# A conditioned attention and expert layer on one core: expert products spread one per step behind the scores, and one mask product per head

## The reference

```
x = x + attention(layernorm(x), ...)        # 16 heads of 64, one shared key and value head
x = x + experts(x, ...)                     # 8 experts of 128, the best 2 per token, and a shared one of 256

attention:  q = l2norm(xn @ Wq) * q_scale;  k = l2norm([null_k, xn @ Wk]) * k_scale
            sim = 8 * q @ k.T + relative position bias
            sim = -max where key > query, and where mask is false
            out = layernorm(softmax(sim) @ [null_v, v] @ Wout)

experts:    y = sum over the 2 chosen experts of weight * (leaky(x @ Wgate) * (x @ Wup)) @ Wdown
            y = y + the same without a weight for the shared expert (two blocks of 128)
```

## Time and profile before

| | |
|---|---|
| three runs | 1165.67, 1167.64, 1169.62 us |
| the profiled execution | 1168.08 us, span 1166.3 us |
| PE busy | 1052.0 us, 90% of the span |
| DVE busy | 776.0 us, 67% |
| ACT busy | 526.6 us, 45% |
| POOL busy | 443.6 us, 38% |
| mean granted PE clock | 0.972 |

### The profile page before, as it was taken

One profiled execution on the slowest core, in us unless ns is written; L12 is line 12 of the kernel. 1 busy time (PEld: TensorE's weight loads), 2 busy tenths in 40 slices (PEclk: granted clock), 3 DMA queues, 4 the chain that ended last, 5 costly groups with the idle time before them and its releaser, 6 DMA issues.

```text
span 1166.3 us, 23102 instructions
## 1 busy us (share of the span) xinstructions
PE 1052.0 (90%) x7596; PEld 859.3 (74%) x7596; DVE 776.0 (67%) x2538; ACT 526.6 (45%) x1563; POOL 443.6 (38%) x422
## 2 busy tenths in 40 slices
PE   2477898999989999999999999899999999999888
PEld 1366697778877787777877788777877779777777
DVE  7768758775677648675586756776486756866443
ACT  2057725553346514655255533465146552566111
POOL 3154423542434405453235424344154533354212
PEclk9678999999999999999999999999999999999989
DMA  5154312221122112222122211221122121221033
GB/s 198 34 157 164 137 37 73 84 82 55 38 83 91 64 40 73 73 64 64 57 73 83 82 55 38 83 91 64 38 74 74 67 62 37 86 97 57 36 104 113
DMA packets 40843, 89.89 MB, mean 77 GB/s; under 512 B 4016, under 2 KB 18880, under 8 KB 40208
## 3 DMA queue, kind: packets, MB, share of 16 engines
q1 hardware_dynamic: 40720, 88.28, 23.5%
HBM read 78.67 MB, written 11.70 MB: 77 GB/s over the span
## 4 chain that ended last, share of the span: by engine, by line
PE 64%; DVE 21%; issue 8%; ACT 3%; POOL 1%; SPq 1%; DMA 1%; DVEq 0%; POOLq 0%; ACTq 0%
PE psY L1456 10%; PE psS L1355 7%; PE psG L60 6%; PE psG L62 5%; PE psO L1389 5%; PE psG L61 5%; DVE work L1038 3%; PE psT L1370 3%; PE psS L60 2%; PE psS L61 2%; PE psS L62 2%; PE psO L1392 2%; DVE work L1044 2%; PE psT L60 2%; PE psT L62 2%
## 5 line engine op out<-in xcount | busy, mean ns | idle before, releaser
L548 POOL TENSOR_TENSOR work<-work,rden 128x514 f32<-128x514 f32 x128 | 134.3, 1049 | 359.0 <-DVE rden L1019 359.0
L671 ACT ACTIVATE work<-work,low 128x257 f32<-128x257 f32 x256 | 128.3, 503 | 110.4 <-DVE low L1038 109.5
L1456 PE MATMUL psY<-Wd,H 128*128 128x256 f32 x640 | 156.7, 388 | 0.0
L1456 PEld LDWEIGHTS psY<-Wd,H 128*128 128x128 f32 x640 | 116.3, 189 | 22.6 <-issue 8.4
L1038 DVE CUSTOM_DVE_ANT_0 work<-psS,bias,null_s 128x256 f32<-128x256 f32 x256 | 113.1, 478 | 28.3 <-PE psS L1359 27.4
L1355 PE MATMUL psS<-KB_hi,qT_hi 64*128 64x256 f32 (+1 forms) x512 | 92.7, 351 | 43.3 <-DVE low L1044 36.6
L1128 DVE SCALAR_TENSOR_TENSOR leaky<-leaky 128x512 f32<-128x512 f32 x80 | 58.8, 735 | 103.3 <-ACT leaky L703 102.3
L60 PE MATMUL psG<-x1T_hi,Wgu 128*128 128x512 f32 x280 | 127.0, 453 | 0.1
L535 POOL TENSOR_TENSOR rq<-qss,neghalf 128x16 f32<-128x16 f32 x32 | 93.7, 2929 | 52.4 <-DVE qss L1013 52.4
L62 PE MATMUL psG<-x1T_lo,Wgu 128*128 128x512 f32 x280 | 112.2, 401 | 0.0
L61 PE MATMUL psG<-x1T_hi,Wgu 128*128 128x512 f32 x280 | 111.1, 397 | 0.0
(11 more groups left out here) (242 smaller groups left out, 2759.6 us busy)
## 6 DMA issues: line engine op xcount, KB each, us to landing
Wgu<-wexp SPq DMA_DIRECT2D x80, 512.0 KB, 3.3
Wb<-wscr SPq DMA_DIRECT2D x64, 256.0 KB, 3.5
wexp<-Wgu SPq DMA_DIRECT2D x10, 512.0 KB, 2.9
xin<-in_x SPq DMA_DIRECT2D x8, 512.0 KB, 5.8
xres<-in_x SPq DMA_DIRECT2D x8, 512.0 KB, 4.4
out<-work SPq DMA_DIRECT2D x8, 512.0 KB, 3.1
H<-in_wgu SPq DMA_DIRECT2D x10, 256.0 KB, 3.3
bscr<-bscr SPq DMA_DIRECT2D x1, 2048.0 KB, 12.7
```

The source lines that it names most:

```text
L548: pool.tensor_tensor(T1[sl][:, hs, :], T1[sl][:, hs, :], rden[sl][:, 1, hs].unsqueeze(2) .to_broadcast([P, 2, N + 1]), ALU.mult)
L671: act.activation(T1[sl][:, h, :], T1[sl][:, h, :], ACT.Exp, scale=-1.0, bias=low[sl][:, 1, h:h + 1], accum_out=den[sl][:, 1, h:h + 1])
L1456: mm = te.matmul(psY[:, t // 2, (t % 2) * D:(t % 2 + 1) * D], H[:, k % H_RING, t * P:(t + 1) * P], Wd[:, ORDER[k], :], start=(k == 0 and t ...
```

## The change

Five things are changed.

1. `score` does the mask first and once per head: `MK` is laid out so that 256 + 128 columns stand beside each other, and one product of 384 columns replaces one of 256 and one of 128. DVE builds `MK` from 768 instead of 512 columns, and four mask DMAs replace two.
2. The tables: `gate` and `up` begin one step earlier, `down` of block 1 moves before step 0, and most `down`s are cut in halves of two token tiles and placed in two neighbouring steps. `weigh` has a table of its own.
3. Within a step PE does `score`, then `up` or `gate`, then `value`, `turn_q`, `down` and `turn` (before: `score`, `value`, `turn_q`, `down`, `gate`, `up`, `turn`).
4. ACT does `exps` and `take_gate` first and `head_out` after them (before: `head_out` first). DVE does `hidden` directly after `scores`, then `turned_q`, `leak` and only then `head_out` (before: `head_out` directly after `scores`). This holds in round 0 too.
5. The router product `logits` moves behind the first half of the third query tile.

```diff
+GATE_AT = {0: 3, 2: 4, 4: 5, 6: 6, 9: 7, 11: 8, 13: 9}
+UP_AT = {1: 3, 3: 4, 5: 5, 7: 6, 10: 7, 12: 8, 14: 9}
...
+DOWN_AT = {4: (2, FIRST), 5: (2, SECOND), 6: (3, FIRST), 7: (3, SECOND), 8: (4, WHOLE), 9: (5, FIRST), 10: (5, SECOND),
+           11: (6, FIRST), 12: (6, SECOND), 13: (7, FIRST), 14: (7, SECOND), 15: (8, FIRST), 16: (8, SECOND), 18: (9, WHOLE)}
...
@@ scalar engine, one step @@
-                    if n >= VALUE_LAG:
-                        head_out(r, n - VALUE_LAG)
                     if n < ALL:
                         exps(r, n // STEPS, n % STEPS)
                     if moe is not None and n in GATE_AT:
                         take_gate(moe, GATE_AT[n])
+                    if n >= VALUE_LAG:
+                        head_out(r, n - VALUE_LAG)
...
@@ vector engine, one step @@
                         scores(r, n // STEPS, n % STEPS)
-                    if n >= VALUE_LAG:
-                        head_out(r, n - VALUE_LAG)
+                    if moe is not None and n in UP_AT:
+                        hidden(moe, UP_AT[n])
                     for u in UNITS_AT.get(n, ()):
                         turned_q(r, u)
                     if moe is not None and n in GATE_AT:
                         leak(moe, GATE_AT[n])
+                    if n >= VALUE_LAG:
+                        head_out(r, n - VALUE_LAG)
...
@@ matrix engine, before the steps @@
+                need(te, qs_done, r, 1)
+                q_half(2, 0)
                 if moe is not None:
                     logits(moe)
-                need(te, qs_done, r, 1)
-                q_half(2, 0)
...
-                    down(moe, 0)
+                    down(moe, 0, WHOLE)
+                    down(moe, 1, WHOLE)
@@ matrix engine, one step @@
+                    if moe is not None:
+                        if n in UP_AT:
+                            up(moe, UP_AT[n])
+                        if n in GATE_AT:
+                            gate(moe, GATE_AT[n])
                     if n >= VALUE_LAG:
                         value(r, n - VALUE_LAG)
...
                         if n in DOWN_AT:
-                            down(moe, DOWN_AT[n])
-                        if n in GATE_AT:
-                            gate(moe, GATE_AT[n])
-                        if n in UP_AT:
-                            up(moe, UP_AT[n])
+                            down(moe, *DOWN_AT[n])
...
@@ score @@
+                for i in range(2):
+                    half = slice(i * DH, (i + 1) * DH)
+                    te.matmul(psS[:, i, 0:N + P], pick_bf[half, :], MK[half, bb, :], start=True, stop=False)
                 for first, q1, keys_ in ((0, q0 + P, N), (N, q0, P)):
                     for a, b in ((0, 0), (1, 0), (0, 1)):
...
-                    for i in range(2):
-                        half = slice(i * DH, (i + 1) * DH)
-                        mm = te.matmul(psS[:, i, first:first + keys_], pick_bf[half, :], MK[half, q0:q0 + keys_],
-                                       start=False, stop=True, skip_group_check=True)
```

More of the change, by code:

```diff
@@ L50 @@
 UNITS_AT = {0: (4, 5), 2: (6, 7)}
-GATE_AT = {1: 3, 3: 4, 5: 5, 7: 6, 10: 7, 12: 8, 14: 9}
-UP_AT = {n + 1: k for n, k in GATE_AT.items()}
-DOWN_AT = {2: 1, 4: 2, 6: 3, 9: 4, 11: 5, 13: 6, 16: 7, 18: 8, 19: 9}
+GATE_AT = {0: 3, 2: 4, 4: 5, 6: 6, 9: 7, 11: 8, 13: 9}
+UP_AT = {1: 3, 3: 4, 5: 5, 7: 6, 10: 7, 12: 8, 14: 9}
+WEIGH_AT = {2: 2, 3: 3, 4: 4, 6: 5, 8: 6, 10: 7, 12: 8, 14: 9}
+FIRST, SECOND, WHOLE = range(0, 2), range(2, 4), range(0, 4)
+DOWN_AT = {4: (2, FIRST), 5: (2, SECOND), 6: (3, FIRST), 7: (3, SECOND), 8: (4, WHOLE), 9: (5, FIRST), 10: (5, SECOND),
+           11: (6, FIRST), 12: (6, SECOND), 13: (7, FIRST), 14: (7, SECOND), 15: (8, FIRST), 16: (8, SECOND), 18: (9, WHOLE)}
 def products(te, dst, a, b, start, stop):
@@ L156, in attention_moe @@
         KB = [sb(f"KB_{part}", [P, BB, N], F32R) for part in PARTS]
-        MK = sb("MK", [P, TOK], BF16)
-        mask8 = sb("mask8", [P, TOK], U8)
+        MK = sb("MK", [P, BB, N + P], BF16)
+        mask8 = sb("mask8", [P, BB, N + P], U8)
         T_SIZE = 2 * GH * (N + 1 + P + 1)
@@ L296, in attention_moe @@
         xres_in = events("xres_in", 16)
-        mask_in = events("mask_in", 32)
+        mask_in = events("mask_in", 64)
         wscr_in = events("wscr_in", 16, 16)
@@ L414, in load_round @@
                 for i in range(2):
-                    sp.dma_start(mask8[i * DH:i * DH + 1, :], mask[:, bass.ds(r * TOK, TOK)]).then_inc(mask_in.sem, 16)
+                    for a, b in ((0, N), (N, P)):
+                        sp.dma_start(mask8[i * DH:i * DH + 1, :, a:a + b],
+                                     mask[:, bass.ds(r * TOK, TOK)].rearrange("a (b j) -> a b j", b=BB)[:, :, 0:b]) \
+                            .then_inc(mask_in.sem, 16)
                 need(sp, x1_done, r - 1, TILES)
@@ L540, in attention @@
                     sl, hs = g % 2, slice(2 * st, 2 * st + 2)
-                    if moe is not None and n in UP_AT:
-                        if UP_AT[n] == SHARED + 1:
-                            weigh(moe, SHARED)
-                        weigh(moe, UP_AT[n])
+                    if moe is not None and n in WEIGH_AT:
+                        weigh(moe, WEIGH_AT[n])
                     if n == NORM_AT + 1 and following is not None:
@@ L889, in attention @@
                 ins.then_inc(kd_done.sem, 1)
-                need(dve, mask_in, r, 32)
+                need(dve, mask_in, r, 64)
                 dve.tensor_scalar(MK[:], mask8[:], -BIG, BIG, ALU.mult, ALU.add).then_inc(mk_done.sem, 1)
@@ L943, in attention @@
                         ch.end()
-                    if moe is not None and n in UP_AT:
-                        hidden(moe, UP_AT[n])
                     if moe is None and 0 <= n - 3 < BLOCKS:
@@ L1354, in score @@
                             half = slice(i * DH, (i + 1) * DH)
-                            te.matmul(psS[:, i, first:first + keys_], qT[a][half, p, q1:q1 + P], KB[b][half, bb, 0:keys_],
-                                      start=(a + b == 0), stop=False, skip_group_check=True)
-                    for i in range(2):
-                        half = slice(i * DH, (i + 1) * DH)
-                        mm = te.matmul(psS[:, i, first:first + keys_], pick_bf[half, :], MK[half, q0:q0 + keys_],
-                                       start=False, stop=True, skip_group_check=True)
+                            mm = te.matmul(psS[:, i, first:first + keys_], qT[a][half, p, q1:q1 + P],
+                                           KB[b][half, bb, 0:keys_], start=False, stop=(first == N and b == 1))
                 mm.then_inc(s_ps.sem, 1)
@@ L1445, in up, with down @@
                 gate_up(m, k, 1, up_bank(k, alone)).then_inc(u_ps.sem, 1)
-            def down(m, k):
+            def down(m, k, tiles):
                 if k < SHARED:
@@ L1454, in down @@
                     need(te, ysum, m - 1, TILES)
-                for t in range(TILES):
+                for t in tiles:
                     mm = te.matmul(psY[:, t // 2, (t % 2) * D:(t % 2 + 1) * D],
@@ L1460, in down @@
                         mm.then_inc(down_ps.sem, 1)
-                if k < BLOCKS - 1:
+                if k < BLOCKS - 1 and tiles[-1] == TILES - 1:
                     mm.then_inc(h_used.sem, 1)
@@ L1482, in _ @@
                 if k >= 2:
-                    down(m, k - 2)
-            down(m, BLOCKS - 2)
-            down(m, BLOCKS - 1)
+                    down(m, k - 2, WHOLE)
+            down(m, BLOCKS - 2, WHOLE)
+            down(m, BLOCKS - 1, WHOLE)
 def kernel(**a):
```

## The result

The changed kernel takes **1199.62 us** (1198.35 to 1201.69, four runs), against 1166.85 for the kernel before beside it: 1.0279 times as long, interval 1.0255 to 1.0303, so slower by 32.8 us. The forecast was 1183, slower by 15. The direction was right and the size less than half. The profiled execution has a span of 1197.8 us, 31.5 more than before.

The account below looks back on a forecast made before the run. It took two chains, PE's work and the loop scores, exponentials, copy, DVE, the loop longer from step 5 on. 1168.1 + 15 (round 0) + 1 (rounds with experts) - 2 (router) + 1 (round 7) gave 1183 us, range 1161 to 1203.

Parts of the forecast that it names:

- the +1: Rounds 1 to 6, with experts: each changes by -0.2 to +1.0, say +0.2, six times, so +1 us.
- The bound of round 0: Round 0: DVE's `head_out` waits 1.75 us for ACT's late copy in 11 steps, nothing hides it; +15 us, bounds 8 and 19.3.
- the score at 0.9 us: Mask pair in `score`: standing first, with 0.9 us from it to the next operation.
- the two waits of `up(3)` and `up(4)`: Head of the steps: `up(3)` waits some 1.7 us for the gate copy, and `up(4)` 2.3 us.
- `value` waiting for the copy of `psO` behind step 15: Rounds with experts: `value` of step 16 waits for `head_out` of step 15.
- Its sign for round 0: Round 0 in the changed profile: starts of `score` should lie at least 4.5 us apart.
- the comparison of the two chains from step 5 on: Round 4, scores of step 5 to 16: DVE's 53.9 us outlast PE's 52.1, so the mask gain goes into waits.
- PE's sum of 52.1 us: PE's own work from step 5 to 16 of round 4: 53.4 us, and 52.1 without a pair of mask products each.
- the 53.9 that I had for the other chain: DVE's time, in the chain through ACT, from the scores of step 5 to those of step 16 in round 4.
- The first steps: Steps 0 to 5 of round 4: old waits filled, `up` waits new, step 5 comes 0.6 us earlier.
- rival 3: PE's clock falls more often, two more falls in each of seven rounds, 3 us a round: 1204 us; chance 0.12.
- The -2 for the router product: Ahead of the router product: PE's 0.64 us wait filled, some 0.55 back; -2 us over seven rounds, bounds 0 and -4.

Follow-up runs that it names:

- `a_round0`: The changed kernel with `head_out` moved back ahead of the exponentials (ACT) and directly behind the scores (DVE) in round 0 alone: 1186.32 us.
- `a_early`: The changed kernel with `head_out` moved back to its early place on ACT and DVE in all rounds, PE's order as changed: 1174.52 us.
- `b_mask`: The kernel before with only the mask edit, one product of 384 columns per head standing first, and its larger mask tile: 1153.70 us.
- `a_oldmask`: The changed kernel with the mask as before, two products a head, last in the score: 1208.49 us.
- `b_logits`: The kernel before with one mask product and the router product behind the first half of the third query tile: 1153.29 us.
- `a_vfirst`: The changed kernel with `head_out` early on ACT and DVE and PE's old order in a step, new tables kept: 1131.63 us.
- section 4: Runs on PE's order within a step; the changed kernel with only that order put back, `head_out` still late, took 1200.78 us.
- `c_tq`: The changed kernel, `head_out` late, with only the query transposes moved on PE to directly behind the scores: 1184.93 us.

## Why the forecast was too low

| part | forecast | measured | by |
|---|---|---|---|
| late copy, round 0 | +15 | +13.3 | `a_round0` |
| late copy, rounds 1 to 7 | in the +1 | +11.8 | `a_early` |
| mask product | 0 (in waits) | -12.8; -8.9 in the change | `b_mask`, `a_oldmask` |
| router product | -2 | about 0 | `b_logits` |
| tables and halves | in the +1 | -22 | `b_logits` to `a_vfirst` |
| order in PE's step, with early copy | in the +1 | +43 | `a_vfirst` to `a_early` |

The rows without the -8.9 add up to +33. They are measured along one path. As section 4 shows, the last one would be near zero if it were taken away first.

**Right.** The bound of round 0 and its mechanism; the score at 0.9 us; the two waits of `up(3)` and `up(4)`; `value` waiting for the copy of `psO` behind step 15. That round 0 came out at +15 is in part luck: the forecast had all of it in steps 5 to 15, which gave 12.5 (`a_round0` to the change), and 3.7 came from behind step 15. Its sign for round 0, starts of `score` at least 4.5 us apart, failed in three of the ten distances (3.3 to 4.0).

**The step that failed** is the comparison of the two chains from step 5 on: "The chain through ACT is the longer one, and PE's gain on the mask goes into waits." PE's sum of 52.1 us was too small, and its work was not covered: in steps 5 to 15 of round 4 PE waits 1.5 of 51.7 us (round 3: 2.9 of 52.6), and in `a_oldmask` each step without a wait is longer by the whole 0.12 of the mask pair. The distances in it were those of the old neighbours. With the ones of the changed trace, 9 expert products of 1.58, ten halves of 0.97 and a whole `down` of 1.83, eleven times 0.91 + 0.80 + 0.75, and 0.6 for the null columns make 53.4. That is level with the 53.9 that I had for the other chain; that two level chains each let the other's delays through is my reading, which no run isolates. Round 7 shows PE's work nearly bare, as it has no norms on DVE: its steps 5 to 15 take 50.9 us, 4.0 more than before, with 1.4 of waits; eight of the ten distances are 5.0 to 5.2. Round 7 also pays 2.0 us ahead of step 5, most of it ahead of step 0, where `down(1)` met no long wait to fill.

**Mis-sized besides.** The first steps. The forecast had step 5 of round 4 come 0.6 us earlier, counted from `turn_x` of its round, and it came 1.2 later (71.15 against 69.92), though both waits were nearly as long as forecast: they are followed by two falls of the clock, 1.8 us, which the walk did not hold, although had shown a fall in just this stretch. Without these it would be the 69.3 of the forecast. In rounds 3 and 6, at full clock, step 5 comes 69.2 us after `turn_x`; round 6 of the kernel before, at full clock too, had 69.0. I priced falls only in rival 3, which came true in part: five falls of 0.9 us, not fourteen of 1.5. The Trainium skill (TensorE: Matmul & The Clock Gate, HAM oscillation) names this pattern, waits between bursts behind which the clock falls again, on a kernel with waits of 3 to 5 us; the rows above agree that it also happens behind 1.5 and 2.1 us, but not every time. `c_tq`, whose waits there are 0.8 and 0.7 us and which has no fall, is 14.7 us faster; how much of that are the falls alone was not isolated, and five of 0.9 would be 4.5. The -2 for the router product, about 0 in `b_logits`, is the other mis-sized term.

**What I did not see at all** is how much there was to lose and to gain inside "+1". The new tables, and the place of the `down`s alone, save more than 20 us. The order of the step gives it back, since a gate of 1.5 us ahead of the query transposes and of `value` holds up the ACT queue that PE then waits for. My walk added both into one number for each step, which came out at +1 for rounds 1 to 6 and +1 for round 7; the rows of the table for these rounds, with the mask product, come to +20.

## What to carry to other kernels

When work is spread into the gaps of a loop, put the product whose result feeds the busiest hand-over (here `value` and the query transposes, whose copies stand ahead of the exponentials) ahead of the filler, and the filler behind it: the same tables ran at 1129.6 and 1157.4 us with `value` ahead of the filler and behind it. Test coupled edits in both orders; a late copy cost 25 us behind one order of PE and 69 behind the other. And when two chains come out within a few per cent of each other, price each edit as if it were on the longer one.

## What the runs showed of the hardware

- Joining a 256- and a 128-column product into one of 384 columns, on both heads, saved 12.8 us for 128 scores, each with one pair of products less: 0.10 us a pair. By the distances a score takes 0.91 us and not 1.03. The Trainium skill (TensorE: Matmul & The Clock Gate, Back-to-back issue gap) gives columns over 2.4 GHz plus 2.5 ns as the distance of isolated products, by which the same columns would take nearly the same time; here the measurement decides against it. The same section says that this formula counts too little for short products with a weight load ahead of each, about 56 ns against 81 measured for 128 columns, and the trace agrees in the direction: a pair of 128 columns takes 0.11 us to the next start, a pair of 256 columns 0.12. The forecast took the formula and not this sentence.
- The same four products of half a `down` (256 columns each) start 0.97 us ahead of the next operation between `value` and a transpose, and 0.86 between an expert product and a transpose, all without a wait and at full clock.
- Waits of 1.5 and 2.1 us of PE were followed by stretches at 1.2 GHz in some rounds and not in others, with the same instructions: 0.86, 0.93 and 1.00 of the full clock in rounds 4, 1 and 3.
